# Moving ScalarE's normalisation steps and Silu runs inside the turn of a conditional Mamba kernel

## The reference

```python
h = _layernorm(x, gamma, beta) * (1.0 + scale[:, None, :]) + shift[:, None, :]
h = h[:, perm]                              # rows taken by an index
xm, z = split(h @ W_in)                     # 1024 channels each
xm = silu(causal_conv4(xm))                 # 4 taps along the sequence
dtr, Bm, Cm = split(xm @ W_xp)
dt = softplus(dtr @ W_dt + b_dt)
# for each of 16 states: hst = hst * exp(dt * A) + (dt * x) * B ;  y += hst * C
y = (y + xm * D_param) * silu(z)
return x + gate[:, None, :] * (y @ W_out)[:, inv_perm]
```

## Time and profile before

| what | value |
|---|---|
| median of 3 runs | 3051.52 us (3049.32 to 3053.63) |
| the profiled execution's own time | 3049.41 us |
| its span, first to last instruction | 3047.6 us |
| PE busy | 2683.2 us (88%) |
| DVE busy | 2372.6 us (78%); 90% or more in nearly all slices of the second layer |
| POOL busy | 1874.2 us (61%) |
| ACT busy | 1604.3 us (53%) |
| first scan of turn 0, of turn 7 | at 1069.7 us, at 2764.2 us |

### The profile page before, as it was taken

The page is one execution under the profiler, slowest core; times in us unless marked ns, Lnnn a source line. Parts: engine busy times, 40 slices in busy tenths (PEclk is TensorE's granted clock), DMA queues, the critical chain, the costliest instruction groups (busy, mean ns, idle before and its releaser), DMA issues. The chain is left out here.

```text
span 3047.6 us, 32689 instructions
## 1 busy us (share of the span) xinstructions
PE 2683.2 (88%) x11046; PEld 1526.8 (50%) x11046; DVE 2372.6 (78%) x3071; ACT 1604.3 (53%) x2412; POOL 1874.2 (61%) x822
## 2 busy tenths in 40 slices
PE   8999999999999877988988988888898898897974
PEld 3556466466465444554554455454455455454542
DVE  3455454455454489999999999999999998999993
ACT  1222223223222465875775776677676687587550
POOL 0112111221223087888899799799799899889991
PEclk9999999999999977999989999999999998998976
DMA  6012022212214344464675665575566566566653
GB/s 213 7 56 77 28 104 90 90 55 89 89 56 152 120 96 98 103 127 112 151 162 118 144 157 120 134 165 128 130 158 141 125 150 144 125 143 141 163 128 74
DMA packets 261596, 355.29 MB, mean 117 GB/s; under 512 B 21597, under 2 KB 115937, under 8 KB 261434
## 3 DMA queue, kind: packets, MB, share of 16 engines
q1 hardware_dynamic: 202024, 246.38, 26.3%
q0 software_dynamic: 55680, 105.93, 19.9%
q10 hardware_dynamic: 3730, 0.96, 0.2%
HBM read 215.56 MB, written 71.58 MB: 94 GB/s over the span
## 5 line engine op out<-in xcount | busy, mean ns | idle before, releaser
L1986 POOL TENSOR_TENSOR hs<-slots,b_wide 128x2048 f32<-128x2048 f32 x255 | 1268.9, 5003 | 142.8 <-PE bank L1514 140.7
L2173 DVE TENSOR_TENSOR_SCAN hs<-bank,hs 128x512 f32<-128x512 f32 x1024 | 1218.6, 1208 | 26.4 <-ACT bank L1759 22.1
L1759 ACT ACTIVATE bank<-dt,decay 128x512 f32<-128x512 f32 x1022 | 699.0, 691 | 542.2 <-DVE hs L2173 537.5
L1514 PE MATMUL bank<-ident,hs 128*128 128x128 f32 x4096 | 676.4, 294 | 250.0 <-DVE acc L2191 186.3
L1514 PEld LDWEIGHTS bank<-ident,hs 128*128 128x128 f32 x4096 | 513.7, 150 | 736.0 <-issue 265.4
L2191 DVE SCALAR_TENSOR_TENSOR acc<-bank,c_t,acc 128x512 f32<-128x512 f32 x772 | 560.8, 727 | 48.5 <-PE bank L1514 40.7
L1466 PE MATMUL bank<-h_t,w_in 128*128 128x512 f32 x1024 | 508.1, 605 | 1.5 <-ACT h_t L1679 1.4
L2034 POOL DMA_DIRECT2D acc<-scaled x252 | 289.0, 1147 | 49.4 <-DMA acc<-scaled 29.3
L1562 PE MATMUL bank<-w_y,zs 128*128 128x512 f32 x512 | 254.6, 603 | 1.3 <-DVE zs L2291 1.3
L1477 PE MATMUL bank<-w_out,h_in 128*128 128x512 f32 x448 | 222.1, 620 | 4.0 <-ACT dt L1726 3.5
L803 PE MATMUL bank<-z_t,w_k 128*128 128x512 f32 x512 | 221.2, 592 | 0.9 <-ACT z_t L902 0.9
(11 more groups left out here) (167 smaller groups left out, 3100.4 us busy)
## 6 DMA issues: line engine op xcount, KB each, us to landing
b_wide<-b_rows SPq DMA_DIRECT2D x256, 256.0 KB, 3.6
acc<-scaled POOLq DMA_DIRECT2D x252, 256.0 KB
w_in<-in_L_cond_W_in SPq DMA_DIRECT2D x128, 256.0 KB, 4.7
z<-in_x SPq DMA_DIRECT2D x8, 2048.0 KB, 9.0
res<-in_x SPq DMA_DIRECT2D x8, 2048.0 KB, 9.3
h_tiles<-h_t SPq DMA_DIRECT2D x56, 256.0 KB, 2.8
h_in<-h_tiles SPq DMA_DIRECT2D x56, 256.0 KB, 5.3
x_rows<-w_part POOLq DMA_DIRECT2D x28, 512.0 KB, 6.6
```

The costliest lines, as they stand in the source:

```text
L1514: last = nc.tensor.transpose(bank[:, j * P:(j + 1) * P], hs[:, slot, j, t * P:(t + 1) * P], ident[:, :])
L1759: nc.scalar.activation(decay_banks[N % 3][:, :], dt[:, H % 2, j, :], ACT.Exp, scale=g.decay[:, 4 * (H % 2) + j, s:s + 1]).then_inc(da_read ...
L1986: nc.gpsimd.tensor_tensor(hs[:, U % RING, :, :], slots[:, H % SLOTS, :, :], b_wide[:, U % B_RING, :].unsqueeze(1).to_broadcast([P, 4, CHUNK]),
L2173: nc.vector.tensor_tensor_scan(block, decay_banks[N % 3][:, :], block, 0.0, ALU.mult, ALU.add).then_inc(scanned, 1)
```

## The change

The four shifts move from step 14 to step 18. The normalisations, four in a row at step 15, go one each to steps 19, 20, 21, 22; each waits for its own shift. The second Silu run on z moves from step 2 to 3, the first on x from 45 to 43, the third on x from 74 to 75; the second and the fourth stay at 63 and 83. Now all five begin in a step with n % 4 == 3, behind the scaling. Silu on z at 104 is unchanged.

```diff
-SILU_Z_AT = (104, 2)
+SILU_Z_AT = (104, 3)
-NORM_AT = 15
+NORM_AT = (19, 20, 21, 22)
-SILU_X_AT = (45, 63, 74, 83)
+SILU_X_AT = (43, 63, 75, 83)
-SHIFT_AT = 14
+SHIFT_AT = 18
-def rows_normed_by_act(nc, g, n, it):
-
-    need(nc.scalar, g.shift_ready, CT * n)
-    for t in range(CT):
-        nc.scalar.activation(g.rows[:, t, :], g.rows[:, t, :], ACT.Identity, scale=g.rs[:, t:t + 1], bias=g.shift[:, t:t + 1]).then_inc(g.normed, 1)
+def rows_normed_by_act(nc, g, n, t):
+
+    need(nc.scalar, g.shift_ready, CT * (n - 1) + t + 1)
+    nc.scalar.activation(g.rows[:, t, :], g.rows[:, t, :], ACT.Identity, scale=g.rs[:, t:t + 1], bias=g.shift[:, t:t + 1]).then_inc(g.normed, 1)
-                        if n == NORM_AT:
-                            rows_normed_by_act(nc, g, b + 1, b + 1)
+                        for t, at in enumerate(NORM_AT):
+                            if n == at:
+                                rows_normed_by_act(nc, g, b + 1, t)
```

## The result

The changed kernel takes 3059.41 us (median of 9 runs, 3056.57 to 3062.15) against 3051.52 before: ratio 1.0026, 95% interval 1.0017 to 1.0034, so 5 to 10 us slower. The forecast was 3058. The profiled execution took 3059.85 us (span 3058.0), 10.4 us more than the one profiled before.

The account below looks back on a forecast made before the run. VectorE was taken as the busiest engine, but GpSimd's chain as setting scan 32 in turns 2 to 6. Terms +10.7 + 0.7 - 5.1 = +6.3 us on the 3051.5 median gave 3058 us, range 3047 to 3065.

Parts of the forecast that it names:

- Silu at 75: Step 77, turns 0 to 6: VectorE's tap waits 1.5 us for ScalarE's late first tap, 10.7 us lost in all.
- Silu on z at 3: TensorE's 2.96 us scaling wait, low clock and waits of steps 6, 9, 11 go; scan 7 waits 1.28 us.
- Shifts and normalisations: Shifts at 18, normalisations at 19 to 22: the 1.06 us wait and those of steps 18 to 20 go, nothing replaces them.
- Turns 2 to 6 keep nothing: VectorE reaches scan 32 about 5 us sooner but waits there for GpSimd; worth 0.2 us in all.
- Turn 1 and turn 7: GpSimd's margin at scan 32 is 2.5 and 2.0 us, so gains of 2.2 and 2.0 us count.
- The gains together: Gains up to scan 32: turn 1 2.2, turn 7 2.0, turn 0 0.75, turns 2 to 6 0.2; 5.1 us.
- Silu on x at 43: Scan 47's decay: nothing lost, by 0.08 us, except in turn 0, which loses 0.7 us with a later addition.
- the sum's 6.3: Whole kernel: +10.7 for the tap, +0.7 for Silu on x at 43, -5.1 of gains, so +6.3 us.
- B: Rival: GpSimd moves along at scan 32, turns 2 to 6 give up to 24 us, 3034 us; chance 0.10.
- C: Rival: the tap at step 77 doesn't wait, only small gains are left, 3047 us; chance 0.12.
- D: Rival: scan 32's wait idles TensorE, half clock and a late addition follow, up to 14 us; 3063 us; chance 0.15.
- E: Rival: turns 1 and 7 lose their gains, their GpSimd chains also nearly closed; 3062 us; chance 0.13.

Follow-up runs that it names:

- two different edits: Changed kernel with third Silu run on x back at step 74: 3049.16 us; changed kernel with VectorE's last taps one step later: 3048.11 us.
- the later tap: Changed kernel, Silu still at 75, VectorE's taps of the last channel group one step later (78 in place of 77): 3048.11 us, 0.9985.
- the three runs on the tap: Changed kernel, third Silu on x back at 74: 0.9996; kernel before, only that run moved to 75: 1.0044; changed kernel, last taps a step later: 0.9985.
- the same transfer: GpSimd's fourth W-product adding transfer, unit 6 to 10: kernel before 3046.59 us; changed kernel with third Silu on x at 74, 3040.36 and 3040.97 us.

## Why the prediction was right, step by step

- **Silu at 75, +10.7 us.** Right: seven waits of 1.47 us, 10.3 by the waits. From scan 77 to scan 78 pass 3.98 us in place of 2.41, so 1.57 a turn, 11.0 in all. Taking it away by two different edits brought back 10.3 and 11.3 us by the medians, 12.5 and 11.0 in the second layer.
- **Silu on z at 3.** Right in the waits: scan 7 waits 1.29 us in turns 1 to 7, against 1.28 worked out, and TensorE's 2.96 us wait for the scaling is gone. Wrong in a cause: the low clock was put down to that wait, and was to go with it. It came ahead of the wait. TensorE in turn 4, before, with its stretch at the lower level (columns as in the earlier trace rows):

```profile
2040.10 0.66 PE L1514 MATMUL bank<-ident,hs 128*128 128x128 f32 x4 [1.12 <-DVE acc L2191]
2041.96 1.09 PE L1514 MATMUL bank<-ident,hs 128*128 128x128 f32 x4 [1.21 <-DVE acc L2191]
```

```profile
2041.70:2051.80 10.10, 6.87 (x19) 4.33 (x20) 8.79 (x10) 6.73 (x8) 9.19 (x6) 0.50 0.89 162
```

  The four matmuls at 2041.96 already take 1.09 us in place of 0.66; the wait of 2.96 us begins at 2043.05. In each of turns 1 to 7 the low level began 0.7 to 3.9 us ahead of that wait, during or just behind the second or third of some shorter waits, of 1.1 to 1.3 us each, for VectorE's additions. Those waits are still there after the change, and so is the low level, in all seven turns. Turn 4, after:

```profile
2047.09 1.94 PE L1513 MATMUL bank<-ident,hs 128*128 128x128 f32 x8 [1.21 <-DVE acc L2191]
2049.88 1.12 PE L1513 MATMUL bank<-ident,hs 128*128 128x128 f32 x4 [0.86 <-DVE acc L2191]
2050.79 3.62 PE L1476 MATMUL bank<-w_out,h_in 128*128 128x512 f32 x4
```

```profile
2045.80:2055.90 10.10, 8.04 (x22) 4.91 (x22) 8.81 (x11) 8.97 (x10) 9.49 (x6) 0.50 0.87 166
```

  What became shorter is the wait of step 9: 0.96 us in turn 4, 0.27 in turn 3, 0.20 in turn 6, next to nothing in turns 1, 2, 5 and 7 (before, 0.97 to 2.5). The low stretch was 10.2 us long in turns 3, 4 and 6 and 6.8 in the four others; before it was 10.2 in all but turn 3, the turn with the shortest wait. So the scaling's wait was one part of the wait at step 9. The other lies with the low clock, in which the four matmuls at 2050.79, ahead of step 9's tile, take 3.62 us; the change doesn't take it away. In turns 2 to 6 that costs nothing, in turn 1 it does (below).
- **Shifts and normalisations.** The shifts wait for nothing (the row below, to set beside the earlier trace rows), and most of the waits of steps 18 to 20 go; waits of 0.2 to 0.3 us remain at step 18 in turns 2 to 4, and 1.2 us at 17 in turn 2. They cost nothing, since scan 32 waits anyway. New are waits of the moments for the gathered rows at step 11, 0.2 to 1.0 us in four turns.

```profile
2079.41 0.85 ACT L436 ACTIVATE shift<-rs,mean_neg 128x1 f32<-128x1 f32 x4
```

- **Turns 2 to 6 keep nothing.** Right, and the point on which the sign hung. From the inputs of unit 27 to the end of unit 8's inputs GpSimd takes 1986.65 to 2098.80 = 112.2 us before and 1991.76 to 2104.30 = 112.5 us after, turns 3 to 4; in eight profiles of seven kernels (before, after and those of the third run, Silu on z, the shifts alone and the later tap), whatever VectorE did, that stretch lay between 111.0 and 114.5 us in turns 2 to 6. The kernel with everything but the run at 75 kept at most a few us of what VectorE saved there. GpSimd after, the two ends (the second ends at 2104.30):

```profile
1991.76 4.55 POOL L1986 TENSOR_TENSOR hs<-slots,b_wide 128x2048 f32<-128x2048 f32 x1 [0.43 <-PE bank L1513]
...
2098.73 5.57 POOL L1986 TENSOR_TENSOR hs<-slots,b_wide 128x2048 f32<-128x2048 f32 x1
```

- **Turn 1 and turn 7.** Turn 1: -0.7 us, the forecast -2.2 + 1.5. Turn 7: -1.6 in place of -2.0; the wait of step 30 grew from 1.16 to 1.43 us. That both came out so closely is in part luck. Up to scan 32 turn 1 took 58.5 us after and 60.7 before, the forecast 2.2; in six other profiles of kernels with both edits it took 59.3 to 59.9, a gain of 0.8 to 1.4, and in most of them additions still wait at step 9 of turn 1 (0.28 to 0.79 us). Turn 7 took 282.3 to 284.1 us in these, against 283.4 before. The gains together were put at 5.1 us, or 4.4 once the 0.7 of Silu on x at 43 is taken off; the kernel with all edits but the run at 75 is faster by 1.2 us by the ratio (from 4.0 faster to 1.5 slower), and by 2.6 in the second layer. So the large term, the tap, carried the forecast, and the small ones may be too large.
- **Where the size was off.** Turns 2 to 6 grew by 10.5 us, 7.4 were forecast. These 3.1 us, with 0.4 in turn 7 and 0.5 in the first layer, make up the span's 10.4 against the sum's 6.3. Some 0.2 of them are the tap, 0.6 steps 88 to 100. The rest, 2.2, lies in the chain's stretch, which was taken as fixed and was 0.4 us a turn longer. GpSimd's waits for its adding transfers are 37.0 us, before 29.3, 30 times in place of 24:

```profile
POOL acc L2034 <- DMA acc<-scaled: 37.0, 30, 3.2
```

  That these waits made the chain longer isn't shown: with the third run at 74 they are 38.5 us, and the chain is as short as before. 0.4 us a turn is also what two profiles of one kernel, the shifts and normalisations alone, differ by. The two kernels in which the tap waits have the longest chains of the eight profiles, 566.4 and 566.0 us over turns 2 to 6, the others 562.0 to 565.2; why wasn't tried. The medians, 7.9 us apart, lie nearer to the sum.
- **Rivals.** B (GpSimd moves along) is out by the runs of Silu on z alone, of the shifts alone, and of all edits but the run at 75; C (no tap wait) by the three runs on the tap. D (TensorE idle at scan 32) was right in its mechanism and wrong in its cost. Behind scan 32 of turn 4, after, TensorE is busy for 4.14 of 6 us (before, from scan 32 on, for all of 6.1):

```profile
2104.00:2110.00 6.00, 4.14 (x16) 1.91 (x15) 5.60 (x7) 2.77 (x4) 6.00 (x5) 1.00 0.78 139
```

  It waits there for VectorE's addition in each of turns 2 to 6: 0.76, 2.79, 1.65, 2.78 and 2.76 us, and in none of them before. The granted clock stays at 1.00 behind the first and the third, and falls to 0.50 for 3.4 us behind the three of 2.8 us. TensorE in turn 3, after, and the stretch at the lower level:

```profile
1863.26 0.65 PE L1513 MATMUL bank<-ident,hs 128*128 128x128 f32 x4 [2.79 <-DVE acc L2191]
1864.12 3.04 PE L1465 MATMUL bank<-h_t,w_in 128*128 128x512 f32 x4 [0.21 <-ACT h_t L1678]
```

```profile
1864.90:1868.10 3.20, 3.20 (x8) 1.71 (x7) 3.20 (x5) 0.89 (x3) 3.20 (x3) 0.50 0.69 134
```

  But no late addition follows: from behind scan 32 up to scan 76 VectorE waits nowhere in turns 1 to 6. E (turns 1 and 7 lose their gains): in this profile they kept them but for 0.4 us; in those of the other kernels with both edits turn 1 kept about half of its gain up to scan 32 and turn 7 between nothing and 1.1 us.

## What to carry to other kernels

Ahead of moving work off a waiting engine, look for the next place where that engine meets another one's queue, and how much margin is there: up to scan 32, 31 of the 46 us that VectorE waited for others than GpSimd went and 9 came back at scan 7, yet without the run at 75 the kernel is only 1 to 3 us faster, because GpSimd's queue met VectorE at scan 32 with 0.1 us to spare. Where an instruction is moved by one step, the price is read at everything that stands behind it on its queue within its length, here a first tap two steps on. The two are worked on together: the same transfer moved out of GpSimd's stretch gave 3 us before the waits were taken from VectorE and 8 after it, and both together gave the fastest version, 3040.4 us, 0.9962 of the kernel before. And before a low clock is put down to a wait, compare when each began.

## What the runs showed of the hardware that was not expected

TensorE's granted clock fell to 0.50 in steps 2 to 4 of every turn from 1 to 7, before and after, at waits of only 1.1 to 1.3 us each, two or three of them in a row with short work between; the longest wait of that place, 2.96 us, began after the fall. After the change it fell behind scan 32 where TensorE had waited 2.8 us, and not where it had waited 0.76 or 1.65 us.

The first scan, behind code that is the same in every kernel, came up to 4.2 us apart between profiled executions (1066.8 to 1071.0 us); in the three earliest the clock was low for 13.4 to 13.6 us ahead of it, in the others for 14.5 to 20.4. The second layer of one and the same kernel differed by up to 5.3 us (1977.7 and 1972.4). So leaving out the first layer takes away one part of the scatter only, and a difference of a few us needs the medians of many executions.

Taking an issue of 1.65 us a turn out of GpSimd's stretch and packing the others closer didn't shorten that stretch (112.2 us on average, against 111.2 and 111.5), while its waits for landings were 38.2 us in all, against 30.6 and 33.4.
